# A routed two-expert feed-forward on 128-token tiles: bias folded into W1, and the split of the normalised token moved to GpSimd

## The reference

```
x = x + conv_ref(ln_c(x))           # layer norm over channels, a 3x3 depthwise kernel made from
                                    # the image's mean and maximum, plus bias, plus its input
t = tokens(x)                       # 32768 tokens of 128
u = ln_t(t)
top 2 of 8 experts by u @ Wg + bg; weights: softmax of the two
h_e = gelu(u @ W1[e] + b1[e])       # 128 -> 512, exact GELU
t = t + sum over the two of w_e * (h_e @ W2[e] + b2[e])   # 512 -> 128
```

## Time and profile before

| | |
|---|---|
| median of 3 runs | 1923.3 us (1921.19 to 1933.44) |
| span of the profiled execution, first to last instruction | 1798.2 us |
| median less that span | 125.1 us |
| TensorE busy, mean granted clock over the span | 1536.5 us (85%), 0.939 |
| VectorE, ScalarE, GpSimd busy | 1396.4, 1202.0, 866.1 us |

### The profile page before, as it was taken

How to read it: one execution, slowest core, us unless ns; L and a number is a source line. 1 busy time by engine, 2 the same in 40 slices (tenths; PEclk the granted TensorE clock), 3 DMA queues, 4 the chain that set the end, 5 groups by cost and what they waited for, 6 DMA issues and landing times.

```text
span 1798.2 us, 45758 instructions
## 1 busy us (share of the span) xinstructions
PE 1536.5 (85%) x12335; PEld 1186.0 (66%) x12336; DVE 1396.4 (78%) x2440; ACT 1202.0 (67%) x2949; POOL 866.1 (48%) x905
## 2 busy tenths in 40 slices
PE   5889999999999519999999999999999999999665
PEld 2445555555555307878888778878777788878555
DVE  0468888788788737888888888888888888888644
ACT  3466667767666308878777887788777887888400
POOL 1003455355355464555555555555555555555500
PEclk8899999999998659999999999999999999999965
DMA  3211121121121061111111111111111111110099
GB/s 120 59 35 56 54 72 59 59 70 60 61 58 49 31 146 30 39 39 36 42 42 37 36 38 39 39 40 35 41 42 37 40 38 42 42 37 22 22 374 359
DMA packets 90626, 115.76 MB, mean 64 GB/s; under 512 B 15286, under 2 KB 71794, under 8 KB 90583
## 3 DMA queue, kind: packets, MB, share of 16 engines
q1 hardware_dynamic: 65784, 62.29, 12.2%
q0 software_dynamic: 18176, 34.27, 5.5%
q10 hardware_dynamic: 6624, 18.69, 2.8%
HBM read 60.22 MB, written 58.61 MB: 66 GB/s over the span
## 4 chain that ended last, share of the span: by engine, by line
issue 31%; POOL 28%; PE 24%; ACT 7%; DMA 4%; DVE 4%; POOLq 1%; SPq 0%; ACTq 0%; DVEq 0%
POOL token_out L454 12%; POOL yt L449 9%; PE psV L731 8%; POOL yt L447 6%; DMA ye<-token_out 4%; PE psR L703 3%; PE psV L691 3%; ACT spent L531 2%; PE psA L682 2%; PE psT L716 2%; PE psR L747 2%; PE psG L718 1%; POOL rows_by_pair L439 1%; DVE x L963 1%; ACT sq L508 1%
## 5 line engine op out<-in xcount | busy, mean ns | idle before, releaser
L1138 DVE TENSOR_TENSOR gl<-g,gh 128x1024 f16<-128x1024 f32 x312 | 438.1, 1404 | 70.5 <-ACT gh L624 65.2
L439 POOL DMA_INDIRECT rows_by_pair<-rows,idx x256 | 265.0, 1035 | 393.3 <-issue 245.4
L454 POOL DMA_INDIRECT token_out<-yt,rt x312 | 323.1, 1036 | 184.6 <-POOL yt L449 133.5
L616 ACT ACTIVATE g<-psV,b1col 128x256 f32<-128x256 f32 x624 | 244.4, 474 | 143.6 <-PE psV L825 143.6
L616 ACT ACTIVATE g<-psT,b1col 128x256 f32<-128x256 f32 x624 | 244.4, 474 | 53.4 <-PE psT L825 53.4
L731 PE MATMUL psV<-lp,diag 128*128 128x512 f32 x512 | 254.2, 626 | 24.8 <-ACT cv L524 14.6
L823 PE MATMUL psV<-xh,wall 128*128 128x256 f16 x624 | 171.9, 275 | 94.6 <-DVE xl L1128 53.8
L447 POOL TENSOR_TENSOR yt<-ya 128x256 f32<-128x256 f32 x156 | 112.9, 724 | 247.0 <-DVE ya L1150 246.9
L841 PE MATMUL psG<-wall,gh 128*128 x1248 | 222.7, 273 | 1.7 <-DVE ya L1146 1.4
L841 PE MATMUL psR<-wall,gh 128*128 x1248 | 222.7, 273 | 0.7 <-DVE ya L1150 0.7
L842 PE MATMUL psG<-wall,gl 128*128 x1248 | 214.3, 219 | 0.0
(11 more groups left out here) (187 smaller groups left out, 3254.9 us busy)
## 6 DMA issues: line engine op xcount, KB each, us to landing
rt<-rows_by_pair SPq DMA_DIRECT2D x156, 133.0 KB, 2.1
xb<-in_x_dram SPq DMA_DIRECT2D x32, 512.0 KB, 3.5
ye<-token_out SPq DMA_DIRECT2D x32, 512.0 KB, 9.1
out_dram<-oe ACTq DMA_DIRECT2D x32, 512.0 KB, 5.8
token_out<-yt,rt POOLq DMA_INDIRECT x312, 2.3
rows_by_pair<-rows,idx POOLq DMA_INDIRECT x256, 2.4
stage<-in_L_ffn_W_dram SPq DMA_DIRECT2D x1, 2048.0 KB, 12.3
rows_by_pair<-pad_rows SPq DMA_DIRECT2D x15, 133.0 KB, 5.2
```

What stands on the lines that cost most here:

```text
L439: gp.indirect_dma_start(rows_dram, bass.IndirectOffsetOnAxis(ap=idx[p][:, b:b + 1].bitcast(U32), axis=0), rows[p][:, b, :], None).then_inc ...
L454: gp.indirect_dma_start(y_dram, bass.IndirectOffsetOnAxis(ap=rt[r][:, b, ID:ID + 1].bitcast(U32), axis=0), yt[r][:, b, :], None, bounds_ch ...
L616: last = sc_.activation(g[side][:, s * T:(s + 1) * T], hbank[side][:, s * T:(s + 1) * T], ACT.Gelu, bias=b1col[:, bass.ds(e * HS + s, 1)], ...
L1138: v.tensor_tensor(gl[side][:, :], g[side][:, :], gh[side][:, :], ALU.subtract).then_inc(lo_done, 1)
```

## The change

Tiles have 128 rows, so NT is 284, and every buffer of the expert stage has one block. The rings are 12 slots long, 12 tiles make a pass of the loop, the first 12 and the last 20 tiles are written out. Each of g, gh, gl has two buffers a side, psA and psV hold two tiles of `up` a side, and TensorE works on tile j+2's products up between tile j's down. GpSimd normalises six tiles ahead, makes both 16-bit halves in the token's own layout (`xs`) and scatters; TensorE transposes both halves in f16 into one bank, and ScalarE copies both out at once (`xt`). Products down have 128 columns each, high and low half of W2 apart, and b2 comes first. VectorE adds both experts and the token in two operations.

b1 is folded: the row's NMR has 1 added, so the normalised token is u + 1, and W1 has (its column sum - b1) / 128 subtracted, by products with ones and with -b1 (`shift_bank`) behind the image stage; since u has mean zero, (u + 1) @ W1' is u @ W1 + b1. W2 and b2 are split in the image stage's first step, W1 only after the shift. The pad rows, the table's T and the start-up's b1 transposes change with it (not shown).

```diff
-    T = 2 * P
-    TB = T // P
+    T = P
     CAP = NTOK + 2 * T
     OFF = [a * (2 * E - a - 1) // 2 for a in range(E - 1)]
     NT = NTOK // T + NPAIR
...
-    RING = 6
-    assert NT % RING == 0 and RING % 6 == 0
+    RING = 12
+    LOOPS = NT // RING - 1
+    AHEAD = 6
+    assert RING % 4 == 0 and LOOPS > 1
...
+        rt = [sb(f"rt{r}", [P, RW]) for r in range(RING)]
+        xn = [sb(f"xn{q}", [P, D]) for q in range(4)]
+        xs = [sb(f"xs{q}", [P, 2, D], F16) for q in range(4)]
+        xt = [sb(f"xt{q}", [P, 2, P], F16) for q in range(4)]
+        g = [[sb(f"g{side}{q}", [P, H]) for q in range(2)] for side in range(2)]
+        gh = [[sb(f"gh{side}{q}", [P, H], F16) for q in range(2)] for side in range(2)]
+        gl = [[sb(f"gl{side}{q}", [P, H], F16) for q in range(2)] for side in range(2)]
+        ya = [sb(f"ya{q}", [P, D]) for q in range(2)]
+        yt = [sb(f"yt{r}", [P, D]) for r in range(RING)]
...
-        hbank = (psV, psT)
-        ybank = (psG, psR)
+        hbank = lambda side, r: (psA, psV)[side][:, H * (r % 2):H * (r % 2 + 1)]
+        xbank = lambda r: psT[:, 512 * (r % 2):512 * (r % 2) + P].bitcast(F16).rearrange("p (n t) -> p n t", n=2)
+        ybank = lambda side: (psG, psR)[side][:, 0:D]
+        shift_bank = [bank[:, half:half + H] for bank in (psA, psV, psT) for half in (0, 512)] + [psG[:, :], psR[:, :]]
...
-                    sp.wait_ge(y_out[r], 16 * TB * t)
+                    sp.wait_ge(y_out[r], 16 * t)
...
+            def normalise(j, r, t):
+                q = r % 4
+                pool.wait_ge(row_in[r % RING], 16 * (t + r // RING + 1))
+                pool.sem_inc(row_seen, 1)
+                gp.tensor_scalar(xn[q][:, :], rt[r % RING][:, 0:D], rt[r % RING][:, RSTD:RSTD + 1], rt[r % RING][:, NMR:NMR + 1], ALU.mult, ALU.add).then_inc(xn_done, 1)
+                pool.wait_ge(xn_done, j + 1)
+                if not isinstance(j, int) or j >= 4:
+                    pool.wait_ge(xT_ready, j - 3)
+                pool.sem_inc(turn_seen, 1)
+                gp.tensor_copy(xs[q][:, 0, :], xn[q][:, :]).then_inc(xh_done, 1)
+                pool.wait_ge(xh_done, j + 1)
+                gp.tensor_tensor(xs[q][:, 1, :], xn[q][:, :], xs[q][:, 0, :], ALU.subtract).then_inc(xl_done, 1)
+            def scatter(j, r):
+                pool.reg_alu(tiles, tiles, 2, ALU.add)
+                pool.wait_ge(s_const, 3)
+                pool.wait_ge(ya_done, tiles)
+                gp.indirect_dma_start(y_dram, bass.IndirectOffsetOnAxis(ap=rt[r][:, ID:ID + 1].bitcast(U32), axis=0),
+                                      yt[r][:, :], None, bounds_check=NTOK - 1, oob_is_err=False).then_inc(y_out[r], 16)
+            for j in range(AHEAD):
+                normalise(j, j, 0)
+            for j in range(RING):
+                normalise(j + AHEAD, j + AHEAD, 0)
+                scatter(j, j)
...
+                    normalise(RING * t + r + AHEAD, r + AHEAD, t)
+                    scatter(RING * t + r, r)
...
+            for e in range(E):
+                act.wait_ge(s_shifted, e + 1)
+                sc_.activation(wall_e[:, e, O_1H:O_1L], stage_1[:, e, :], ACT.Copy, scale=WSCALE).then_inc(s_high, 1)
+            def high(j, r):
+                act.wait_ge(xT_ready, j + 1)
+                if not isinstance(j, int) or j >= 4:
+                    act.wait_ge(h_ready, 2 * j - 6)
+                sc_.activation(xt[r % 4][:, :, :], xbank(r), ACT.Copy).then_inc(xt_done, 1)
+            def gelu(j, side, r):
+                act.wait_ge(h_ready, 2 * j + side + 1)
                 if not isinstance(j, int) or j >= 2:
+                    act.wait_ge(lo_done, 2 * j + side - 3)
+                sc_.activation(g[side][r % 2][:, :], hbank(side, r), ACT.Gelu, scale=1.0 / WSCALE).then_inc(g_done, 1)
                 if side == 1:
                     act.wait_ge(g_done, 2 * j + 2)
+                    if not isinstance(j, int) or j >= 2:
+                        act.wait_ge(y_ready, 2 * j - 2)
+                    sc_.activation(gh[1][r % 2][:, :], g[1][r % 2][:, :], ACT.Copy).then_inc(hi1_done, 1)
+            def dstep(j, r):
+                last = isinstance(j, int)
+                if not last or j + 2 < NT:
+                    gelu(j + 2, 0, r)
+                if not last or j + 4 < NT:
+                    high(j + 4, r)
+                if not last or j + 2 < NT:
+                    gelu(j + 2, 1, r)
...
+            for e in range(E):
+                te.matmul(shift_bank[e], ones[:, :], stage_1[:, e, :], start=True, stop=False)
+                te.matmul(shift_bank[e], ident[0:E, e:e + 1].broadcast_to([E, P]), b1n[:, :], start=False, stop=True).then_inc(s_shift, 1)
...
             def turn_rows(j, r):
-                pe.wait_ge(xn_done, j + 1)
+                pe.wait_ge(xl_done, j + 1)
                 if not isinstance(j, int) or j >= 2:
-                    pe.wait_ge(xl_done, j - 1)
-                    pe.wait_ge(xh_done, j - 1)
-                for b in range(TB):
-                    last = te.transpose(psA[:, 512 * (r % 2) + b * P:512 * (r % 2) + (b + 1) * P], xn[r % 2][:, b, :], ident[:, :])
+                    pe.wait_ge(xt_done, j - 1)
+                for n in range(2):
+                    last = te.transpose(xbank(r)[:, n, :], xs[r % 4][:, n, :], ident_h[:, :])
                 last.then_inc(xT_ready, 1)
-            def up(j, side, q, o):
-                w = weights(o, side)
-                pe.wait_ge(xh_done, j + 1)
-                pe.wait_ge(xl_done, j + 1)
+            def up(j, side, r):
+                w = weights(r, side)
+                pe.wait_ge(xt_done, j + 1)
+                if not isinstance(j, int) or j >= 2:
+                    pe.wait_ge(g_done, 2 * j + side - 3)
+                for s in range(HS):
+                    out_ = hbank(side, r)[:, s * P:(s + 1) * P]
+                    high = wall[:, bass.ds(w + (O_1H + s * P), P)]
+                    te.matmul(out_, high, xt[r % 4][:, 0, :], start=True, stop=False)
+                    te.matmul(out_, high, xt[r % 4][:, 1, :], start=False, stop=False)
+                    last = te.matmul(out_, wall[:, bass.ds(w + (O_1L + s * P), P)], xt[r % 4][:, 0, :], start=False, stop=True)
+                last.then_inc(h_ready, 1)
+            def down(j, side, r):
+                w = weights(r, side)
+                bank = ybank(side)
                 if not isinstance(j, int) or j >= 1:
-                    pe.wait_ge(g_done, 2 * j + side - 1)
-                for s in range(HS):
-                    out_ = hbank[side][:, s * T:(s + 1) * T]
-                    high = wall[:, bass.ds(w + (O_1H + s * P), P)]
-                    te.matmul(out_, high, xh[q][:, :], start=True, stop=False)
-                    te.matmul(out_, high, xl[q][:, :], start=False, stop=False)
-                    last = te.matmul(out_, wall[:, bass.ds(w + (O_1L + s * P), P)], xh[q][:, :], start=False, stop=True)
-                last.then_inc(h_ready, 1)
-            def down(j, side, o):
-                w = weights(o, side)
+                    pe.wait_ge(ya_done, 2 * j + side - 1)
+                te.matmul(bank, bias_sel[:, :], wall[:, bass.ds(w + O_B2, D)], start=True, stop=False)
                 pe.wait_ge(lo_done, 2 * j + side + 1)
                 pe.wait_ge((hi0_done, hi1_done)[side], j + 1)
-                pe.wait_ge(ya_done, 2 * j + side + 1)
-                bank = ybank[side]
                 for s in range(HS):
-                    both = wall[:, bass.ds(w + (O_2 + 2 * s * D), 2 * D)]
                     high = wall[:, bass.ds(w + (O_2 + 2 * s * D), D)]
-                    for b in range(TB):
-                        lhs = slice(s * T + b * P, s * T + (b + 1) * P)
-                        te.matmul(bank[:, 2 * b * D:2 * (b + 1) * D], gh[side][:, lhs], both, start=(s == 0 and b == 0), stop=False, skip_group_check=True)
-                        te.matmul(bank[:, 2 * b * D:(2 * b + 1) * D], gl[side][:, lhs], high, start=False, stop=False, skip_group_check=True)
-                bias = wall[:, bass.ds(w + O_B2, D)]
-                for b in range(TB):
-                    last = te.matmul(bank[:, 2 * b * D:(2 * b + 1) * D], bias_sel[:, :], bias, start=False, stop=(b == TB - 1), skip_group_check=True)
+                    low = wall[:, bass.ds(w + (O_2 + (2 * s + 1) * D), D)]
+                    toks = slice(s * P, (s + 1) * P)
+                    te.matmul(bank, gh[side][r % 2][:, toks], high, start=False, stop=False)
+                    te.matmul(bank, gh[side][r % 2][:, toks], low, start=False, stop=False)
+                    last = te.matmul(bank, gl[side][r % 2][:, toks], high, start=False, stop=(s == HS - 1))
                 last.then_inc(y_ready, 1)
...
             def dstep(j, r):
+                last = isinstance(j, int)
+                if not last or j + 2 < NT:
+                    up(j + 2, 0, r + 2)
+                if not last or j + 3 < NT:
+                    experts(j + 3, r + 3)
```

(65 more changed lines are left out.)

236 lines of the change are left out of this document (70 added, 166 removed).

## The result

The changed kernel takes 2789.3 us (2786.8 to 2791.3, 4 runs), the kernel before 1925.4 us (4 runs): ratio 1.447, 95% interval 1.443 to 1.452. The forecast was 2695 us with a range of 2570 to 2840. The profiled execution took 2786.8 us, with a span of 2785.0.

What follows compares the result with a forecast made beforehand. TensorE's sequencer, working out weight addresses, was taken as the bound: 284 x 6.3 - 156 x 6.50 = +775 us on a span of 1798.2 gives 2573, plus 125.1 carried over makes 2698, rounded 2695 us; range 2570 to 2840.

Steps and rivals of the forecast that it cites:

- The bound and its reason: Expert stage: TensorE's sequencer, with 34 address operations a tile, sets the pace at 6.3 us; the array needs only 2.9.
- Rival A: Expert stage: the sequencer is not the bound, engines set the pace at 3.3 us a tile, 1846 us; chance 0.06 faster.
- Rival B: Expert stage: weight loads of 98 ns per 128-column matmul set the pace, 5.1 us a tile, 2357 us; chance 0.04.
- Rival C: Expert stage: a slice's third product needs its address again, 42 a tile, 7.3 us, 2982 us; chance of C 0.07.
- The step: TensorE's sequencer: each weight address operation costs 0.13 us, 34 of them 4.4 us a tile.
- The tile: Expert stage: a 128-row tile takes 6.3 us, from addresses 4.4, table load 0.65 and small operations 1.2.
- the small operations: TensorE's sequencer: register snaps and waits, 12 a tile at 0.1 us each, 1.2 us.
- The 125 us "around the span": Whole kernel: the median 1923.3 lies 125.1 us above the profiled span of 1798.2; carried over unchanged to the forecast.
- The wait of the earlier trace: First weight load of `up`, L823: "issue" wait of 0.79 us a tile, read as waiting for nothing on another engine.
- ScalarE, VectorE, GpSimd hidden: Expert stage: 1.9 to 3.8, 1.9 to 5.6 and 3.0 to 4.1 us a tile, all hidden under 6.3.
- The W1 shift at nothing: Behind the routing: 12 us of work inside a 19 us gap before the first row load, costing nothing, from -6 to +16 overall.
- The back-to-back rule: TensorE's array: about 81 ns per 128-column load and matmul pair, so 4.2 us a tile, still under the sequencer's 6.3.

Runs made afterwards that it cites:

- e1: Changed kernel with constant weight addresses (other experts than the table's), no address operations and no table load: 1889.1 us.
- e4: Changed kernel with both halves of W2 in one product of 256 columns, so 8 addresses and 8 products fewer a tile: 2367.1 us.
- e3: Kernel before with 16 more address operations a tile, same products and data: 2052.7 us beside 1923.8.
- e6: Changed kernel with constant weight addresses (other experts than the table's) and GpSimd only normalising: 1678.5 us beside 1880.9 for the kernel before, 0.892.
- the repeat: Kernel before, unchanged, traced a second time: 1911.2 us, span 1909.4.
- g1: Kernel before with experts by the tile's place, no address operations and no table load: 1918.0 us beside 1919.7, ratio 0.996.
- f1: Kernel before with VectorE's subtraction for the tokens' low half moved ahead of its long hidden-layer subtraction: 1826.7 us, ratio 0.972.
- e5: Changed kernel with two more GpSimd additions of 128 x 128 a tile, into spare buffers: 2786.2 us.
- e7: Changed kernel with GpSimd only normalising; TensorE transposes once in f32, ScalarE copies the high half, VectorE subtracts: 2781.4 us.

## Why the prediction was right, and where it was off

- **The bound and its reason** were right. One address operation per distinct address, 34 a tile (34.1 counted), each with the same step whether one or two products follow; e1 took them and the rest of the register work away and 3.25 us a tile went; e4 took 8 away and 1.06 us went; e3 added 16 where they hadn't mattered and they did. Rival A (engines at 3.3 us) describes e1, not the changed kernel. Rival B (weight loads at 0.098 us each) falls with e6: 51 products a tile, each with its own load, in 2.90 us, and with the two equal steps of a slice. Rival C (42 addresses) falls with the count.
- **The step** was 0.13 us in the forecast. It is 0.124 in the median and 0.131 on average: 4.48 us a tile against the forecast's 4.4.
- **The tile** was mis-sized: 6.74 instead of 6.3 us. 0.28 of the 0.44 is the stop at the end of a pass, a term that was not in the sum; the trace of before has no such stop to read. The rest is spread over the three terms that were there: addresses 4.48 for 4.4, the table load 0.72 for 0.65, the small operations 1.26 for 1.2. The 32 written-out tiles were counted like those of the loop and are shorter, 5.96 us at the start and 6.09 us at the end from table load to table load, with fewer small operations. The forecast's 1789 + 22 = 1811 us for the stage was 87 us short.
- **The 125 us "around the span"** were misplaced. I took the difference between a median and another execution's span for a constant around the span. Most of it was the way to the first tile, which was short in that one execution: first row load at 669.2, in the repeat at 774.6, in the changed kernel at 787.0. Against the forecast's 2698 (before rounding) the profiled execution has +117.9 us up to the first row load, +87 in the stage, +6.3 in the last one and -123 around the span: 2786.8. That carrying the 125 us over came out right was luck: other executions have about that time inside, where I hadn't looked for it.
- **The wait of the earlier trace rows** was misread. "Issue" at L823 was not the sequencer in the way of the array: g1 takes all addresses away and the wait stays, now named for GELU. It did no harm to the sum, because the sequencer's sum in the changed kernel was counted and not taken from that wait. It did hide the cheapest gain, f1's.
- **ScalarE, VectorE, GpSimd hidden**: right. In the changed kernel they are busy 36, 43 and 33% of the span; GpSimd's four operations take 204.24 / 89 = 2.3 us a tile, where the forecast had 3.0 to 4.1 with a wait of 0.85 in it. e4, e5 and e7 show the room directly.
- **The W1 shift at nothing**: right, though not under the cover that the forecast names. The gap of 19 us between VectorE's table and the first row load belongs to that one execution: in the repeat the table ends after the last scatter (762.3 and 753.5), and the first row load follows 12.2 us behind the table, as it does in the changed kernel (774.8 and 787.0). There the corrections and splits of W1 run from 774.9 to 784.5, inside those 12.2 us. From last scatter to first row load it is 23.2 us against 21.0 in the repeat, and from there to the first product up (L847, L823) 10.1 against 5.1: some 7 us in all, within the forecast's -6 to +16.
- **The back-to-back rule** of the Trainium skill ("TensorE: Matmul & The Clock Gate", Back-to-back issue gap), 81 ns for a product of 128 columns: e6 disagrees. 2.90 us for 51 products is 0.057 us each at most, and the measurement decides.

## What to carry to other kernels

Where an operand's address comes from a register, count the distinct addresses per tile beside the columns per tile, and multiply by the step that the sequencer shows. Halving the tile halves the columns but not the addresses, and an address that was free behind 256 columns becomes the pace behind 128. And before a wait called "issue" is taken for the engine's own, look at what else that instruction has to wait for; the order of a neighbour's queue may be the cheapest thing to change.

## What the runs showed of the hardware

- A weight address out of a register costs TensorE's sequencer 0.124 us in the median, at a record length of only 46 ns, whether one product follows or two, and alike at a granted clock of 1.2 and of 2.4 GHz (0.131 and 0.132 on average). The load of two registers from SBUF takes 0.72 us of it with its own address, a wait or a register move about 0.1.
- A pass of 12 tiles ends in a stop of 3.3 to 3.9 us with 218 packets on the instruction queue; with 8 tiles, or 12 tiles of 26 addresses, there are 29 and 34 packets and no such stop.
- Products of 128 columns with a load each follow one another at 0.057 us, tile after tile, at a granted clock of 1.00 (e6).
- GpSimd's cast of 128 x 128 takes 289 ns with no VectorE instruction beside it (the changed kernel), 291 beside VectorE's cast or its sum, and 452 to 758 where it overlaps VectorE's subtraction for gl (e1).
- The image stage of one and the same kernel took some 90 us less in one execution than in another, with the granted clock at 0.97 there and 0.88 here from 200 to 300 us. Why the clock was granted differently wasn't tried.
